# A channel gate with a spatial max and mean: gate values moved, discarded matmuls added, and half a tile added by another engine

## The reference

```
n  = groupnorm(x, 32 groups of 16 channels)
r  = relu(n)
r  = 0 where max over pixels - mean over pixels < 0.5      # per channel
bb = 1 - exp(-|max over channels - mean over channels|)     # per pixel
y  = bb * r
pooled   = mean over pixels of y
control1 = sigmoid(pooled @ W1.T)
control3 = relu(pooled @ W3.T);  1.2 where it is < 1
thres    = control1 * control3 * max over pixels of y       # per channel
out = x + (y where y >= thres, else 0)
```

## Time and profile before

| | |
|---|---|
| median of 3 runs | 1694.12 us (1691.63 to 1694.9) |
| the profiled execution | 1694.59 us, span 1692.8 us |
| busy: DVE, ACT, PE, POOL | 1459.9 (86%), 1355.9 (80%), 1266.6 (75%), 610.5 us (36%) |
| mean granted TensorE clock | 0.868 of full |
| HBM traffic | 310.38 MB read, 205.52 MB written, 305 GB/s over the span |
| SyncE transfers | 260 loads and 256 stores of 784 KB, 2 loads of weights |
| GpSimd accumulating transfers | 124 of 784 KB |

### The profile page before, as it was taken

One profiled execution on the slowest core, in us unless ns is written; L12 is line 12 of the kernel. 1 busy time (PEld: TensorE's weight loads), 2 busy tenths in 40 slices (PEclk: granted clock), 3 DMA queues, 4 the chain that ended last, 5 costly groups with the idle time before them and its releaser, 6 DMA issues.

```text
span 1692.8 us, 26138 instructions
## 1 busy us (share of the span) xinstructions
PE 1266.6 (75%) x9888; PEld 883.0 (52%) x9888; DVE 1459.9 (86%) x2192; ACT 1355.9 (80%) x2177; POOL 610.5 (36%) x446
## 2 busy tenths in 40 slices
PE   3788777887777888777788877778877778877761
PEld 1555455555555555455555555555545555555550
DVE  2588889988889898888998888998888989888896
ACT  6788888788888788888878888888888888888821
POOL 0032334442344442244443243443233444224440
PEclk8988888998788998888898888899888899888885
DMA  9259999999999999999999999999999999999973
GB/s 394 112 127 318 340 355 311 291 314 303 338 350 324 287 316 301 339 343 341 299 303 307 316 343 346 299 309 313 311 342 351 318 299 316 292 340 342 302 228 152
DMA packets 93345, 517.64 MB, mean 306 GB/s; under 512 B 10272, under 2 KB 10272, under 8 KB 93216
## 3 DMA queue, kind: packets, MB, share of 16 engines
q1 hardware_dynamic: 75360, 416.38, 61.1%
q0 software_dynamic: 17856, 99.56, 30.1%
HBM read 310.38 MB, written 205.52 MB: 305 GB/s over the span
## 4 chain that ended last, share of the span: by engine, by line
PE 40%; POOL 28%; ACT 20%; DVE 7%; issue 3%; DMA 1%; DVEq 0%; SPq 0%; ACTq 0%
POOL xs L788 25%; PE ps_gate L331 11%; PE ps_gate L298 10%; PE ps_turn L288 8%; ACT rs L482 6%; ACT rs L457 6%; ACT xs L482 4%; PE ps_gate L318 3%; PE ps_gate L360 2%; PE ps_gate L368 2%; POOL rstd L767 2%; PE ps_gate L306 2%; DVE xs L649 2%; ACT junk L433 1%; DVE max_and_mean L632 1%
## 5 line engine op out<-in xcount | busy, mean ns | idle before, releaser
L632 DVE TENSOR_REDUCE max_and_mean<-ps_turn 128x2 f32<-128x1024 f32 x384 | 463.6, 1218 | 31.8 <-PE ps_turn L288 28.1
L288 PE MATMUL ps_turn<-ident,xs 128*128 128x128 f32 (+1 forms) x1600 | 359.6, 311 | 175.2 <-DVE max_and_mean L632 112.0
L788 POOL TENSOR_TENSOR xs<-xs,rs 128x1568 f32<-128x1568 f32 x124 | 433.3, 3531 | 1.8 <-DVE rs L680 1.8
L779 POOL DMA_DIRECT2D xs<-in_x x124 | 111.5, 968 | 889.4 <-DVE xs L680 796.9
L433 ACT ACTIVATE junk<-xs 128x1568 bf16<-128x1568 f32 x256 | 385.4, 1505 | 9.8 <-ACT junk L433 0.4
L318 PE MATMUL ps_gate<-ident,bb 128*128 128x128 f32 (+1 forms) x1600 | 272.2, 332 | 156.3 <-ACT bb L475 150.8
L288 PE MATMUL ps_turn<-ident,rs 128*128 128x128 f32 (+1 forms) x1600 | 345.7, 302 | 0.0
L318 PEld LDWEIGHTS ps_gate<-ident,bb 128*128 128x128 f32 (+1 forms) x1600 | 248.8, 239 | 175.9 <-DVE ymax_parts L649 163.7
L288 PEld LDWEIGHTS ps_turn<-ident,xs 128*128 128x128 f32 (+1 forms) x1600 | 209.0, 155 | 248.2 <-DVE max_and_mean L632 158.4
L649 DVE CUSTOM_DVE_ANT_0 xs<-xs,ps_gate 128x768 f32<-128x768 f32 (+1 forms) x256 | 243.1, 958 | 48.7 <-PE ps_gate L318 48.5
L457 ACT ACTIVATE xs<-xs,shift,rstd 128x3136 f32<-128x3136 f32 x64 | 192.0, 3001 | 86.0 <-POOL shift L771 80.8
(11 more groups left out here) (80 smaller groups left out, 955.7 us busy)
## 6 DMA issues: line engine op xcount, KB each, us to landing
xs<-in_x SPq DMA_DIRECT2D x260, 784.0 KB, 13.7
out<-xs SPq DMA_DIRECT2D x256, 784.0 KB, 8.2
xs<-in_x POOLq DMA_DIRECT2D x124, 784.0 KB, 10.9
rs<-in_L_conv_W SPq DMA_DIRECT2D x2, 1024.0 KB, 17.5
```

The costliest lines, as they stand in the source:

```text
L288: mm = pe.transpose(ps_turn[0:w, n % 2, b - 2 * i, P * t:P * (t + 1)], r_tile(s, t)[:, P * b:P * b + w], ident[:, :])
L632: ins = dve.tensor_reduce(max_and_mean[:, 2 * i:2 * i + 2, 0], ps_turn[:, n % 2, :, :], AX.X, ALU.max)
L779: pool.dma_start(half(x_tile(s - 1, t), h), dram_half(x_tiles, s - 1, t, h), accum_op=ALU.add).then_inc(x_added[(s - 1) % XR][t][h], 16)
L788: pool.tensor_tensor(o, o, half(r_tile(s - 1, t), h), ALU.add).then_inc(added, 1)
```

## The change

- ScalarE: `pool_sum` of range 0 for tiles 0 to 2 and the gate values of group 3 stand ahead of the last relu. Squares of all tiles but the first in `LOAD_ORDER` take a whole tile instead of two halves; `copy_mean_rows` and `copy_means` stand one tile of squares later. The squares' output, which nobody reads, is 8-bit instead of bf16.
- VectorE: all four gates of group 2 stand ahead of `peaks`; `margins` and `find_fails` follow at once, then gate (3, 0), `read_count` and `settle_channels`, then the other three gates.
- TensorE: `keep_clock` issues discarded matmuls of 512 columns: two behind `spread` 2, two behind `spread` 3, one behind `count_fails`. They write the PSUM buffer that `turn(s+1, 0)` will overwrite.
- The first half of tile 1 (`AGAIN`) is no longer completed by an accumulating DMA. SyncE loads its x into `scratch`, and GpSimd adds it as a fifth addition. `scratch` is shared with the squares' output (`junk`) and with `rows`, so that its load waits for `means_ready` and `row_mean_ready`, and ScalarE waits for `again_added`. Its store and reload move to a later place in SyncE's order. `LOAD_ORDER` changes from (2, 0, 1, 3) to (2, 0, 3, 1).
- GpSimd: `affine` has one operation less, since the row means carry the minus sign.

```diff
-LOAD_ORDER = (2, 0, 1, 3)
+AGAIN = 1
+LOAD_ORDER = (2, 0, 3, 1)
...
-        junk = sb("junk", [P, HALF], BF16)
-        rows = sb("rows", [P, C])
+        scratch = sb("scratch", [P, HALF])
+        junk = scratch[:, 0:HW // 4].bitcast(FP8)
+        rows = scratch[:, HALF - C:HALF]
...
+                elif t == AGAIN and h == 0:
+                    sp.wait_ge(again_added, s + 1)
...
+                sp.wait_ge(means_ready, s + 2)
+                if s + 2 < B:
+                    sp.wait_ge(row_mean_ready, s + 3)
+                sp.dma_start(scratch[:, :], dram_half(x_tiles, s, AGAIN, 0)).then_inc(x_again, 16)
                 store(s, 2, 0)
                 store(s, 0, 0)
                 store(s, 0, 1)
                 store(s, 2, 1)
-                store(s, 1, 0)
                 store(s, 1, 1)
                 reload(2, 0)
                 store(s, 3, 0)
...
                 store(s, 3, 1)
-                reload(1, 0)
                 reload(1, 1)
+                store(s, 1, 0)
                 reload(3, 0)
                 reload(3, 1)
+                reload(1, 0)
...
+            def keep_clock(s, n):
+                pe.wait_ge(t_read, NT * s + NT - 1)
+                for _ in range(n):
+                    pe.matmul(ps_turn[:, NT * (s + 1) % 2, 0, :], ident[:, :], wt[:, 0, 0, :], start=True,
+                              stop=True, skip_group_check=True)
...
                 spread(s, 2)
+                keep_clock(s, 2)
                 spread(s, 3)
                 if s + 1 < B:
+                    keep_clock(s, 2)
                     count_fails(s + 1)
+                    keep_clock(s, 1)
...
+            def square_tile(s, n):
                 t = LOAD_ORDER[n]
+                wait_loaded(act, s, t)
+                square(s, t, slice(0, HW), t)
...
+                if s > 1:
+                    act.wait_ge(again_added, s - 1)
                 if has_next:
-                    square_half(s + 1, 0, 0)
+                    square_half(s + 1, 0)
...
                 if has_next:
                     square_tile(s + 1, 1)
+                    square_tile(s + 1, 2)
                 copy_mean_rows(s)
                 if has_next:
-                    square_tile(s + 1, 2)
+                    square_tile(s + 1, 3)
                 copy_means(s)
                 if has_next:
-                    square_tile(s + 1, 3)
                     row_means(s + 1)
...
                 gate_values(s, 2)
-                pool_sum(s, 0, 0)
+                for t in range(3):
+                    pool_sum(s, 0, t)
+                gate_values(s, 3)
                 if has_next:
                     relu(s + 1, RELU_ORDER[3])
-                gate_values(s, 3)
-                for t in range(1, T):
-                    pool_sum(s, 0, t)
+                pool_sum(s, 0, 3)
...
-                gate(s, 2, 0)
-                gate(s, 2, 1)
-                gate(s, 2, 2)
+                for t in range(T):
+                    gate(s, 2, t)
                 if nxt < B:
                     peaks(nxt)
-                gate(s, 2, 3)
-                if nxt < B:
                     margins(nxt)
                     find_fails(nxt)
                 gate(s, 3, 0)
                 if nxt < B:
                     read_count(nxt)
-                gate(s, 3, 1)
-                if nxt < B:
                     settle_channels(nxt)
-                gate(s, 3, 2)
-                gate(s, 3, 3)
+                for t in range(1, T):
+                    gate(s, 3, t)
...
-                steps.step(pool.tensor_tensor(mrs[:, :], gst[:, 0, :], rstd[:, :], ALU.mult))
-                steps.wait()
-                pool.tensor_scalar(shift[:, :], mrs[:, :], -1.0, 1.0, ALU.mult, ALU.mult).then_inc(affine_ready, 1)
+                pool.tensor_tensor(shift[:, :], gst[:, 0, :], rstd[:, :], ALU.mult).then_inc(affine_ready, 1)
...
-                        for h in range(2):
+                        for h in range(1 if t == AGAIN else 0, 2):
                             pool.dma_start(half(x_tile(s - 1, t), h), dram_half(x_tiles, s - 1, t, h),
                                            accum_op=ALU.add).then_inc(x_added[(s - 1) % XR][t][h], 16)
...
+                    o = half(x_tile(s - 1, AGAIN), 0)
+                    pool.wait_ge(x_again, 16 * s)
+                    pool.tensor_tensor(o, o, scratch[:, :], ALU.add).then_inc(again_added, 1)
```

More of the change, by code:

```diff
@@ L6 @@
 F32 = mybir.dt.float32
-BF16 = mybir.dt.bfloat16
+FP8 = mybir.dt.float8e4
 I32 = mybir.dt.int32
@@ L98, in gated_sparsifier @@
         half_neg = sb("half_neg", [P, T])
-        squares = sb("squares", [P, 2, T])
+        squares = sb("squares", [P, T + 1])
         row_sum = sb("row_sum", [P, 1])
@@ L106, in gated_sparsifier @@
         rstd = sb("rstd", [P, T])
-        mrs = sb("mrs", [P, T])
         shift = sb("shift", [P, T])
@@ L151, in gated_sparsifier @@
                    for p in range(XR)]
+        x_again = sem("x_again")
+        again_added = sem("again_added")
         w_loaded = [sem("w1_loaded"), sem("w3_loaded")]
@@ L342, in group_stats @@
                 pe.matmul(ps_group[:, 0, :], group_pick[:, :], row_mean[:, :], start=True, stop=True)
-                pe.wait_ge(squared, 2 * T * (s + 1))
-                for h in range(2):
-                    mm = pe.matmul(ps_group[:, 1, :], group_avg[:, :], squares[:, h, :], start=(h == 0),
-                                   stop=(h == 1), skip_group_check=True)
-                mm.then_inc(group_sums, 1)
+                pe.wait_ge(squared, (T + 1) * (s + 1))
+                first = LOAD_ORDER[0]
+                pe.matmul(ps_group[:, 1, :], group_avg[:, :], squares[:, 0:T], start=True, stop=False,
+                          skip_group_check=True)
+                pe.matmul(ps_group[:, 1, first:first + 1], group_avg[:, :], squares[:, T:T + 1],
+                          start=False, stop=True, skip_group_check=True).then_inc(group_sums, 1)
             def count_fails(s):
@@ L427, in _, with square, square_half @@
             junk_step = Steps(act, squared)
-            def square_half(s, n, h):
-                t = LOAD_ORDER[n]
[L431 to L438, removed]
+            def square(s, t, cols, part):
+                junk_step.wait()
+                junk_step.step(act.activation(junk[:, cols], x_tile(s, t)[:, cols], ACT.Square,
+                                              scale=float(HW) ** -0.5, accum_out=squares[:, part:part + 1],
+                                              saturate=False))
+            def square_half(s, h):
+                t = LOAD_ORDER[0]
+                act.wait_ge(x_loaded[s % XR][t][h], 16 * (s // XR + 1))
+                square(s, t, slice(HALF * h, HALF * (h + 1)), t if h == 0 else T)
+            def square_tile(s, n):
+                t = LOAD_ORDER[n]
+                wait_loaded(act, s, t)
+                square(s, t, slice(0, HW), t)
             def row_means(s):
@@ L443, in row_means @@
                 steps.step(act.activation(junk[:, 0:XCHUNK], ps_rowsum, ACT.Identity,
-                                          scale=1.0 / (PER_GROUP * HW), accum_out=row_sum[:, :]))
+                                          scale=-1.0 / (PER_GROUP * HW), accum_out=row_sum[:, :],
+                                          saturate=False))
                 steps.wait()
@@ L492, in _ @@
             act.wait_ge(consts_ready, 1)
-            for n in range(T):
+            for h in range(2):
+                square_half(0, h)
+            for n in range(1, T):
                 square_tile(0, n)
@@ L507, in _ @@
                 if has_next:
-                    square_half(s + 1, 0, 1)
+                    square_half(s + 1, 1)
                 if s > 0:
@@ L537, in _ @@
                         pool_sum(s, j, t)
+            act.wait_ge(again_added, B - 1)
             copy_control(B - 1)
```

## The result

The changed kernel is 0.9% slower: 1710.21 us (median of 5; 1699.92 to 1710.9) against 1691.63 us for the kernel before on the same chip; the ratio is 1.0088 (95% interval 1.0055 to 1.0121). I had forecast 1669 us and a gain. The profiled execution took 1710.9 us, its span 1709.1.

What follows compares the result with a forecast made beforehand. The chain of waits through each sample's pass of 50.31 us was taken as the bound. A pass of 49.0 + 0.4 = 49.4 us saves 27 us over 30 passes: 1694.6 - 27 + 1.3 = 1669 us, range 1645 to 1698.

Steps and rivals of the forecast that it cites:

- Gate values ahead of the last relu: ScalarE makes group 3's gate values before the last relu; gate (3, 0) starts at 892.85 instead of 894.06, 1.2 us won.
- Settling sooner: VectorE settles bare behind gate (3, 0), taken as 1.15 us; first transposes come at 894.95 instead of 896.17.
- Discarded products covered: TensorE's discarded matmuls, 0.95 us each at the high clock level, end before the work behind them is due, costing nothing.
- I charge this 1.1 us in four passes of ten: 0.4: Clock falls in the new 2.3 us rest before `turn` 2; control products then cost 3.13 instead of 2.02 us.
- The hand-over with a full clock: From `block_max` 0 at 898.0 through `turn` 2 and products to 902.1, logits at 903.8: a pass of 49.0 us.
- The ends: At the start the last tile is squared whole after it lands instead of by halves: 1.3 us more, once.
- Half a tile by reload: One accumulating transfer per sample becomes a plain load: transfer work 48.4 to 46.3 us a pass, room but no time gained.
- Rival (b): Bare settling costs 1.5 us and the clock falls before `turn` 2 in eight passes of ten: 1694 us; chance 0.10.

Runs made afterwards that it cites:

- a1_fill_rest: The changed kernel with two more discarded matmuls between `turn` 1 and `turn` 2: 1670.07 us, ratio 0.9882 to the kernel before.
- a4_four_accumulating: The changed kernel with the half tile completed by an accumulating transfer again, without the fifth addition: 1705.75 us, ratio 1.0083 to the kernel before.
- c1_fill_four_accumulating: The changed kernel with two discarded matmuls added before `turn` 2 and four accumulating transfers a pass again: 1681.68 us, ratio 0.9939 to the kernel before.
- b2_before_gate_values: The kernel before with only ScalarE's order changed, three sums and group 3's gate values ahead of the last relu: 1666.79 us, ratio 0.9847.
- c4_fill_one: The changed kernel with one discarded matmul added between `turn` 1 and `turn` 2: 1669.21 us, ratio 0.9860 to the kernel before.
- a2_settle_behind_gate: The changed kernel with gate (3, 1) put back ahead of `settle_channels`: 1669.02 us, ratio 0.9866 to the kernel before.

## Why the prediction was wrong, step by step

- **Gate values ahead of the last relu**: right. In passes with nothing else in the way, gate (3, 0) and the flag came 1.2 us sooner, to 0.03 us as worked out, and the wait of `peaks` was 0.34 us (forecast 0.4).
- **Settling sooner**: right in kind, a little small. Flag to the next gate is 1.42 us in the mean instead of 1.15. It was 1.24 to 1.29 us in 18 of 30 passes, near my lower end, and 1.4 to 2.1 in the other 12; together 0.27 us a pass over my term.
- **Discarded products covered**: right in the passes with a full clock (the flag never waits there), wrong in 9 of 30, where the flag is 0.4 us late: 0.1 us a pass.
- **"I charge this 1.1 us in four passes of ten: 0.4"**: this is the step that failed. The rest of 2.3 us was foreseen, and measured 2.41. But it takes the clock in nine passes of ten, not four, and the price is about 1.6 us, not 1.1, since `turn` 2 is slow as well as the products. 5.75 - 4.34 = 1.4 us a pass instead of 0.4. The 1.1 was the products' part alone; in the pass that it was read from (products at 951.29), `turn` 2 was slow too, and the copy began 6.46 us behind `top`, against 4.72 in the pass ahead of it.
- **The hand-over with a full clock**: 0.16 us too short. From `block_max` 0 to the copy it measured 4.34 - 0.08 = 4.26 us, where the working had 902.1 - 898.0 = 4.1. The four misses sum to 0.27 + 0.1 + 1.0 + 0.16 = 1.5 us, which is 50.93 - 49.4.
- **The ends**: I added 1.3 us once. The first logits came 2.7 us later than in the kernel before (101.99 against 99.33), but the last pass, which I had left out, took 45.6 us instead of 49.9. Together, and with 0.4 more behind the last logits, that is 1.2 us less, not 1.3 more; why the last pass is shorter was not tested.
- A reading of mine was off: in the pass of the earlier trace rows only `turn` 0 and 1 run slowly. The clock is back at 899.2, and `turn` 2, from 899.61, takes 1.1 us.
- a1_fill_rest confirms the failed step by cure: with that rest filled, the time is 1670.1 us, against my 1669 for a kernel that loses the clock rarely.
- **Half a tile by reload**: right. Nothing of its own (a4_four_accumulating), room for a faster pass (12 us in c1_fill_four_accumulating). My picture of the transfers was too easy, though: with shorter passes loads are late even with the reload, and the transfer engines stand idle while the first store waits.
- Rival (b) named just this pair, bare settling and the lost clock, but priced it to come out even, and its chance of 0.10 was much too low. With what was measured, the same sum gives 49.0 + 0.27 for the settling + 1.4 for the clock + 0.1 for the late flag + 0.16 for the hand-over = 50.9, on the slower side, where the result lies. The rows of before already held the reason: there the time ahead of `turn` 2 was filled by slow turns. The fuller clock made the turns fast, and so made the rest.

What stays open: how much of the gain of b2_before_gate_values, 0.44 us a pass in the clock, would stay in another order; why the settling lengthens; and why, behind the same rest of 2.41 us, three passes of 30 kept the clock.

## What to carry to other kernels

Where work is issued to keep TensorE's clock, list the rests again with everything at full rate: faster work in front of a wait makes the rest longer, and it can move to the place where the clock costs most. Try each edit of a bundle alone; here the move of two calls alone gained 1.5%, while the bundle as a whole lost 0.9%. Put the settling, a branch on a value from memory, behind other instructions of its engine that hide it, with room to spare: behind one gate it showed in the passes where it took longer, behind two it hardly did.

## What the runs showed of the hardware

- A rest of 2.41 us behind 1.9 us of transposes took the clock in 27 of 30 passes; rests of 1.5 us (c4_fill_one, a2_settle_behind_gate) and 0.69 us at the same place never did.
- A discarded pair of 512 columns takes 1.88 us at 2.4 GHz and up to 3.1 when the clock is low for part of it; I had taken 1.9 and 3.6.
- A granted clock nearer to full is no gain in itself: 0.924 after against 0.868 before, and slower; 0.897 in b2_before_gate_values, and faster.
- A square over a whole tile takes 2.82 us, with 8-bit output, where two halves took 2 x 1.51 with bf16 output and a read behind each.
